# First attention stage: scores in 32-row groups and an order skewed over three sequences; layer weights issued by ScalarE

## What is computed

```
# stage one: one pre-norm attention layer, 16 heads of 8 features, causal
xn = layernorm(x)
q, k, v = xn @ Wq.T, xn @ Wk.T, xn @ Wv.T          # 16 heads x 8
s = q @ k.T / sqrt(8);  s[j > i] = -inf
x = x + (softmax(s) @ v) @ Wo.T
# stage two: six layers on layernorm(x); their result is added back to x
h = layernorm(x)
for l in range(6):
    h = local_attention(shift(h), Wqkv[l], ...) @ Wo[l] + h   # 16 heads x 64, windows of 32
    h = gated_ffn(shift(h), W1[l], b1[l], W2[l], b2[l], ...) + h
x = x + h
```

## Time and profile before

| | |
|---|---|
| median of 3 runs | 4060.95 us |
| profiled execution: its time / its span | 4053.12 / 4051.3 us |
| granted TensorE clock, mean | 0.983 |
| PE busy (share of the span) | 3611.0 us (89%) |
| DVE busy | 3103.8 us (77%) |
| ACT busy | 2876.5 us (71%) |
| POOL busy | 2423.2 us (60%) |
| stage one, until stage two's first PE instruction | 543.15 us |

### The profile page before, as it was taken

One profiled execution on the slowest core, in us unless ns is written; L12 is line 12 of the kernel. 1 busy time (PEld: TensorE's weight loads), 2 busy tenths in 40 slices (PEclk: granted clock), 3 DMA queues, 4 the chain that ended last, 5 costly groups with the idle time before them and its releaser, 6 DMA issues.

```text
span 4051.3 us, 97145 instructions
## 1 busy us (share of the span) xinstructions
PE 3611.0 (89%) x34144; PEld 2541.3 (63%) x34144; DVE 3103.8 (77%) x5305; ACT 2876.5 (71%) x4769; POOL 2423.2 (60%) x1603
## 2 busy tenths in 40 slices
PE   6888869999889999899999899999899998999997
PEld 5666646666566666566666566666666665666665
DVE  4656658888778888778888778888788887888885
ACT  3554447777677777677777677777677776777775
POOL 3222246666666666666666666666566665667663
PEclk9999989999999999999999999999999999999998
DMA  1000001111111111111111111111211111111111
GB/s 56 0 0 0 0 12 34 32 32 34 52 41 31 35 35 35 50 38 35 35 34 36 46 42 35 34 35 35 53 35 35 34 34 44 47 35 35 34 33 48
DMA packets 183169, 136.82 MB, mean 34 GB/s; under 512 B 97612, under 2 KB 135888, under 8 KB 182992
## 3 DMA queue, kind: packets, MB, share of 16 engines
q1 hardware_dynamic: 182992, 134.51, 13.7%
HBM read 19.04 MB, written 2.10 MB: 5 GB/s over the span
## 4 chain that ended last, share of the span: by engine, by line
PE 50%; DVE 14%; ACT 11%; SPq 11%; issue 7%; DMA 5%; POOL 1%; DVEq 0%; ACTq 0%; POOLq 0%
PE ps L1136 9%; PE ps L1177 9%; PE ps L1189 8%; SPq L281 5%; PE ps L1230 5%; PE ps L1215 4%; DMA BD<-area 3%; PE ps L1204 3%; PE ps L1240 3%; SPq L283 3%; DVE area L820 3%; ACT kbd L599 2%; DVE lsum L810 2%; DVE mx L799 2%; DVE area L804 2%
## 5 line engine op out<-in xcount | busy, mean ns | idle before, releaser
L1136 PE MATMUL ps<-Wqkv,xsT 128*128 128x512 f32 x2304 | 1124.0, 611 | 93.1 <-DMA Wqkv<-ffn_Wqkv 44.5
L418 POOL TENSOR_TENSOR area<-area,tab 128x512 f32<-128x512 f32 x384 | 490.1, 1276 | 829.9 <-ACT area L575 829.9
L1136 PEld LDWEIGHTS ps<-Wqkv,xsT 128*128 128x128 f32 x2304 | 406.0, 193 | 432.8 <-issue 337.2
L432 POOL TENSOR_TENSOR area<-area,lsum 128x1024 f32<-128x1024 f32 x192 | 365.3, 1903 | 336.1 <-DVE lsum L813 336.1
L568 ACT ACTIVATE area<-ps 128x1024 f32<-128x1024 f32 x384 | 393.6, 1025 | 202.6 <-PE ps L1136 200.4
L419 POOL TENSOR_TENSOR area<-area,tab 128x512 f32<-128x512 f32 x384 | 490.0, 1276 | 0.0
L426 POOL TENSOR_TENSOR AQb<-AQb,area 128x1024 f32<-128x1024 f32 x192 | 449.8, 2365 | 7.5
L426 POOL TENSOR_TENSOR area<-area 128x1024 f32<-128x1024 f32 x192 | 450.5, 2370 | 0.0
L1177 PE MATMUL ps<-BD,area 128*64 128x128 f32 x6144 | 420.3, 279 | 20.8 <-DMA BD<-area 10.1
L1189 PEld LDWEIGHTS ps<-Wo,area 128*128 128x128 f32 x3072 | 375.9, 193 | 94.5 <-issue 93.6
L1177 PEld LDWEIGHTS ps<-BD,area 128*64 128x64 f32 x6144 | 337.3, 138 | 133.3 <-DMA BD<-area 80.1
(11 more groups left out here) (129 smaller groups left out, 7054.9 us busy)
## 6 DMA issues: line engine op xcount, KB each, us to landing
BD<-area SPq DMA_DIRECT2D x1344, 64.0 KB, 2.0
Vx<-area SPq DMA_DIRECT2D x384, 32.0 KB, 1.9
Wqkv<-ffn_Wqkv SPq DMA_DIRECT2D x18, 512.0 KB, 4.5
BB<-area SPq DMA_DIRECT2D x384, 16.0 KB, 1.8
x2s<-x2s SPq DMA_DIRECT2D x96, 56.0 KB, 2.0
Wo<-ffn_Wo SPq DMA_DIRECT2D x6, 512.0 KB, 4.0
W<-ffn_W SPq DMA_DIRECT2D x6, 341.0 KB
x2s<-x2s SPq DMA_DIRECT2D x96, 7.5 KB, 2.0
```

Source lines behind the costliest of these rows:

```text
L418: pool.tensor_tensor(b4[:, :, 0:h], q4[:, :, h:DH], s4[:, :, 0:h], ALU.mult).then_inc((s_bq, s_bk)[j], 1)
L432: pool.tensor_tensor(p3, p3, lsum[:, 1, :].unsqueeze(2).broadcast_to([P, HEADS, 2 * WIN]), ALU.mult).then_inc(s_pn, 1)
L1136: last = mm(PJ[:, b * 512:(b + 1) * 512], xsT[:, par, t * P:(t + 1) * P], Wqkv[:, w0:w0 + 512], start=True, stop=True)
```

## The change

Stage one:

- k is no longer spread over 128 rows for each head. Four heads share the 32 rows of a group, and POOL writes four copies in place of sixteen (`slotmask`), into one of two halves of `KM`; q is kept twice too. A score product takes its operands from 32 rows of both; two heads of different row groups are done together as a pair j, in two neighbouring banks, one for each head. There are eight pairs in place of four groups. The mask is one product of 256 columns for each head of the pair.
- Maxima are taken by pair (256 and 512 elements), exponentials by pair (four instructions).
- The order is skewed further: pairs 0 to 6 of sequence n and two of its transposed blocks are done in step n, pair 7, the other ten blocks and the value sums in step n+1, and turning, dividing, output product and residual in step n+2. ACT copies four blocks out and DVE eight. The output product goes to `TR[1]`, and pairs and value sums use banks 0 to 5. DVE divides only the eight features of each head, not all 32 columns. The loop is unrolled by two.

The start: `ident` is loaded first; PE no longer waits for `Wap` and `rot`; two large memsets of POOL come after its first spread.

The loads of `Wqkv`: ACT issues them, layer 0's before its first step, the others at the last step of a layer: v after `v_evac(n, 1)`, q after `keep_raw(n, 1, 0)`, k after `keep_raw(n, 1, 1)`.

The core of the diff; in the step functions the removed lines are left out.

```diff
-        KM = area3[:, :].rearrange("p (h k) -> p h k", h=HA)
+        KM = area3[:, 0:2048].rearrange("p (b k n) -> p b k n", b=2, k=4)
...
+        AqT = sb("AqT", [P, 2, SEQ])
...
+            a_step(0, 0, True, False, False)
+            a_step(1, 1, True, True, False)
+            with eng.Fori(0, SEQS // 2 - 1) as k:
+                for odd in range(2):
+                    a_step(eng.snap(2 * k + (2 + odd)), odd, True, True, True)
+            a_step(SEQS, 0, False, True, True)
+            a_step(SEQS + 1, 1, False, False, True)
...
+        BY_ACT = ("00", "10", "01", "02")
+        BY_DVE = ("11", "12", "20", "30", "31", "32", "21", "22")
+
+        SCORE_BANK = {j: 2 * s for j, s in ((7, 0), (0, 1), (1, 2), (2, 0), (3, 1), (4, 2), (5, 1), (6, 2))}
+        VALUE_BANK = 0
...
+        def pair_heads(j):
+            return [(2 * (j % 2) + b, j // 2) for b in range(2)]
...
+            sp.dma_start(ident[:, :], c_ident).then_inc(d_c, 16)
             sp.dma_start(xres[:, 0:early, :], x_rows[:, 0:early, :]).then_inc(d_x, 16)
...
+            for src, dst in ((c_causal, causal_f[:, :]), (c_winmask, wmask_f[:, :, :]), (c_headmask, headmask[:, :])):
...
+                sp.dma_start(Wap[32 * g:32 * g + DA, :, :], wo_rows[g]).then_inc(d_wap, 16)
+            sp.dma_start(xres[:, early:, :], x_rows[:, early:, :]).then_inc(d_x2, 16)
+            sp.dma_start(rot[:, :, :, :], c_rot).then_inc(d_rot, 16)
...
-                if at == SEQS - 1:
-                    need_apart(sp, i_sp, s_pv, (layer + 1) * SEQS * TILES)
-                    load_qkv(layer + 1, 2, d_wv)
-                    need_apart(sp, i_sp, s_pq, (layer + 1) * SEQS * TILES)
-                    load_qkv(layer + 1, 0, d_wq)
-                    need_apart(sp, i_sp, s_pk, (layer + 1) * SEQS * TILES)
-                    load_qkv(layer + 1, 1, d_wk)
...
+            def spread_k(n, par):
                 need(pool, a_ke, n + 1)
...
+                need(pool, a_s, NPAIR * (n - 1))
+                pool.tensor_tensor(KM[:, par, :, :], AkT[:, :].unsqueeze(1).broadcast_to([P, 4, SEQ]),
+                                   slotmask[:, :].unsqueeze(2).broadcast_to([P, 4, SEQ]), ALU.mult).then_inc(a_km, 1)
+
+            def a_step(n, par, head, mid, tail):
+                if head:
+                    spread_k(n, par)
+                    if isinstance(n, int) and n == 0:
+                        pool.memset(kbd[:, :, :, :], 0.0).then_inc(i_zero, 1)
+                        pool.memset(BD[:, :, :, :], 0.0).then_inc(i_zero, 1)
...
+            def load_qkv(l, part, done):
+                col = slice(part * INNER, (part + 1) * INNER)
+                act.dma_start(Wqkv[:, col], wqkv[l][:, col]).then_inc(done, 16)
...
+            def a_exp(n, j):
+
+                need(act, a_mx, NPAIR * n + j + 1)
+                for b, (g, k) in enumerate(pair_heads(j)):
+                    h, bank = 4 * g + k, SCORE_BANK[j] + b
+                    act.activation(E0[:, h, :], ps[:, bank, 0:P], ACT.Exp, bias=nmx[:, 0, h:h + 1])
+                    last = act.activation(E1[:, h, :], ps[:, bank, P:P + SEQ], ACT.Exp, bias=nmx[:, 1, h:h + 1])
                 last.then_inc(a_e, 1)
...
+            def a_step(n, par, head, mid, tail):
+                if mid:
+                    a_values(n - 1)
+                if head:
+                    rsqrt_guess(n, a_lnc, a_lnr, mv, lw)
+                if mid:
+                    a_evac(n - 1, "00")
+                    a_evac(n - 1, "10")
+                if head:
+                    a_x_evac(n)
+                if mid:
+                    a_evac(n - 1, "01")
+                if head:
+                    a_qk_evac(n, par)
+                if mid:
+                    need(act, a_t, NBLK * (n - 1))
+                    a_exp(n - 1, 5)
+                    a_exp(n - 1, 6)
+                    a_exp(n - 1, 7)
+                    a_evac(n - 1, "02")
+                if head:
+                    if mid:
+                        need(act, a_t, turned(n - 1, "02"))
+                    a_exp(n, 0)
+                    a_exp(n, 1)
+                    a_exp(n, 2)
                 if tail:
...
+                    rsqrt_guess(n - 2, b_lnc, b_lnr, mvb, lwb)
+                if head:
+                    a_exp(n, 3)
+                    if mid:
+                        need(act, a_t, turned(n - 1, "22"))
+                    a_exp(n, 4)
 
             act.wait_ge(i_zero, 2)
             act.wait_ge(i_guess, 2)
+            load_qkv(0, 0, d_wq)
+            load_qkv(0, 1, d_wk)
+            load_qkv(0, 2, d_wv)
...
                     v_evac(n, 1, par)
+                    if again:
+                        load_qkv(layer + 1, 2, d_wv)
...
                     keep_raw(n, 1, 0)
+                    if again:
+                        load_qkv(layer + 1, 0, d_wq)
...
                     keep_raw(n, 1, 1)
+                    if again:
+                        load_qkv(layer + 1, 1, d_wk)
...
+            def a_max(n, j):
+
+                bank, (g, k) = SCORE_BANK[j], pair_heads(j)[0]
+                hs = slice(4 * g + k, 4 * g + k + 5, 4)
+                need(dve, a_s, NPAIR * n + j + 1)
+                dve.tensor_reduce(nmx[:, 0, hs], ps[:, bank:bank + 2, 0:P], AX.X, ALU.max, negate=True)
+                dve.tensor_reduce(nmx[:, 1, hs], ps[:, bank:bank + 2, P:P + SEQ], AX.X, ALU.max, negate=True).then_inc(a_mx, 1)
...
+                heads = o3[:, :, 0:DA]
+                dve.tensor_tensor(heads, heads, Arl[:, :].unsqueeze(2).broadcast_to([P, 32, DA]), ALU.mult).then_inc(a_mu, 1)
...
+            def a_step(n, par, head, mid, tail):
+                if head:
+                    moments(n, a_lnc, xres[:, tiles_of(n), :], stats, mv)
+                if tail:
+                    a_gather(n - 2)
+                if head:
+                    a_norm(n)
+                if tail:
+                    a_divide(n - 2)
+                if mid:
+                    a_max(n - 1, 5)
+                    a_evac(n - 1, "11")
+                    a_max(n - 1, 6)
+                    a_evac(n - 1, "12")
+                    a_max(n - 1, 7)
                 if tail:
                     a_residual(n - 2)
+                if mid:
+                    a_evac(n - 1, "20")
+                if head:
+                    a_max(n, 0)
+                    a_max(n, 1)
+                if mid:
+                    a_evac(n - 1, "30")
+                if head:
+                    a_max(n, 2)
+                if mid:
+                    for b in ("31", "32", "21", "22"):
+                        a_evac(n - 1, b)
+                if head:
+                    a_max(n, 3)
+                    a_max(n, 4)
                 if tail:
                     x1_norm(n - 2)
...
+                if isinstance(n, int) and n == 1:
+                    dve.wait_ge(d_x2, 16)
...
+            def a_scores(n, j, par):
+                bank = SCORE_BANK[j]
                 for b in range(2):
...
+                    mm(ps[:, bank + b, 0:3 * P].rearrange("p (a k) -> p a k", a=3)[:, 0:3:2, :], ident_h[:, :],
+                       causal[:, P:2 * P].unsqueeze(1).broadcast_to([P, 2, P]), start=True, stop=False, skip_group_check=True)
+                for b, (g, k) in enumerate(pair_heads(j)):
+                    r = slice(32 * g, 32 * g + 32)
+                    mm(ps[:, bank + b, 0:P], AqT[r, par, 0:P], KM[r, par, k, 0:P], start=False, stop=True, skip_group_check=True)
+                for b, (g, k) in enumerate(pair_heads(j)):
+                    r = slice(32 * g, 32 * g + 32)
+                    last = mm(ps[:, bank + b, P:P + SEQ], AqT[r, par, P:SEQ], KM[r, par, k, :],
                               start=False, stop=True, skip_group_check=True)
...
+            def a_step(n, par, head, mid, tail):
+                old = 1 - par
+                if head:
+                    a_turn(n, mid)
+                if mid:
+                    need(pe, a_te, by_act(n - 1, "10"))
+                    a_turned(n - 1, "01")
+                if head:
+                    a_project(n)
+                if mid:
+                    need(pe, a_te, by_act(n - 1, "01"))
+                    a_turned(n - 1, "11")
+                    need(pe, a_oe, n - 1)
+                    a_scores(n - 1, 7, old)
+                    if head:
+                        need(pe, a_ke, n + 1)
+                    a_turned(n - 1, "12")
                 if tail:
+                    if mid:
+                        need(pe, a_td, by_dve(n - 1, "11"))
                     a_output(n - 2)
                 if mid:
...
+                    need(pe, a_e, NPAIR * n - 2)
+                    need(pe, a_td, by_dve(n - 1, "12"))
+                    a_turned(n - 1, "20")
+                if head:
+                    need(pe, a_km, n + 1)
+                    need(pe, a_qe, n + 1)
+                    a_scores(n, 0, par)
+                if mid:
+                    if tail:
+                        need(pe, a_x1, n - 1)
```

(107 more changed lines are left out.)

234 lines of the change are left out of this document (66 added, 168 removed).

## The result

The changed kernel takes 3852.24 us (median of four runs, 3851.92 to 3856.09), against 4060.78 us before (4055.93 to 4066.61): a ratio of 0.9488, 95% interval 0.9472 to 0.9504, 208 us less. The forecast was 3863 us. In the profiled execution stage one gave back 158 us and stage two 39.

The account below looks back on a forecast made before the run. PE was taken to bound stage one, with waits for Wqkv at stage two's layer ends. 143 us from stage one plus 55 from layer ends, 198, took the 4060.95 us median to 3863; 3835 to 3885 by itself, range to 3928 with rivals.

Parts of the forecast that it names:

- The bound: Stage one: PE bounds it, busy 26.5 us of a 31.5 us sequence, with 5.0 us of waits for copies.
- the slack I gave it: Stage one's new period: PE needs 22.4 us, but 23.0 was taken for a sequence, 0.6 more.
- Scores: Stage one, PE: a pair costs 0.22 masks, 0.75 products, 0.28 mode changes, 1.25 us; eight pairs 10.0 against 13.1.
- my lower bound: Score products of a pair: 0.66 us if the two row groups run side by side.
- The rest of PE: Stage one, PE's transposes, value sums, projections and other work besides scores: 12.4 us a sequence.
- DVE: Stage one: DVE's work rises from 18.8 to 20.5 us a sequence through maxima and copies, less a smaller division.
- The order: Stage one's skewed steps: PE never late by over 0.2 us, margins over DVE 0.2 to 0.5; period 23.0 us.
- the 0.6 us that I added for hand-offs: Stage one's period: allowance for narrow margins between PE at 22.4 and DVE at 20.5 us, giving 23.0.
- Start and end: Stage one: 31 + 24 us beside 15 periods of 23.0; stage two starts at 400 against 543.15, 143 us less.
- Layer ends: Stage two: no PE waits for Wqkv with ACT issuing; 11 us less, five times, 55 us (40 to 60).
- The 0.1 taken off for the four other ends: Layer-end saving: 0.1 us subtracted from each end's 12.1 because the other four waited 0.7 us less on the mean.
- Slow rival: Stage one: the clock falls because 32-row tiles and transposes are lighter work, making the kernel slower; chance 0.04.

Follow-up runs that it names:

- both runs: Changed kernel with layer-end Wqkv loads issued by SP again: 3899.5 us, ratio 0.9616; kernel before with only those loads moved to ScalarE: 4000.32 us, ratio 0.9871.
- the other profiles: Five profiles of the changed kernel or variants of it, with the same start and the same or nearly the same period; stage two begins at 389.0 to 390.1 us.

## Why the prediction was right

- **The bound.** PE bounds stage one: right, and without the slack I gave it.
- **Scores.** A pair was to take 1.25 us and takes 1.17. The bounds were wide, 0.75 for the products looks right to 0.01 (0.22 and 0.11, and 0.43), but that is luck. I thought of loads of 128 columns one behind the other, and the 0.11 is part of the change from whole array to tiles (long products first). The products alone are 0.65, my lower bound, and the change is 0.29 to 0.31 against my 0.28: the error of 0.08 a pair is in the products.
- **The rest of PE**: 21.57 - 8 x 1.17 = 12.2, forecast 12.4.
- **DVE**: 19.5 against 20.5. I had added whole recorded lengths, which overlap from one instruction to the next.
- **The order.** The term that was off is the 0.6 us that I added for hand-offs: no gap is left, and DVE takes 0.8 more without one. With my pair and without the margin the period would have been 22.4; the error of 1.4 us a period is 22 us of stage one.
- **Start and end.** Forecast 55 us beside the 15 periods, measured 385.0 - 15 x 21.57 = 61. I had priced the first step at the high clock. It ran at about half pace until 36.1, 14.6 us after the first masks, where with products over all rows the fast pace came after 3: 7 us. First masks came at 21.5, forecast 20.4: ACT's loads cost 6 us, not 1, and the rest of the start was shorter than I had it. Over the stage the two errors leave 158 us gained against 143; with stage two at 389.0 to 390.1, as in the other profiles, it is 153 to 154.
- **Layer ends.** 52 us by both runs, forecast 55. ACT's issues cost it nothing, forecast 1 us an end; the transfers cost the step before the end some 1 to 2 us, which I had not counted. The 0.1 taken off for the four other ends doesn't follow from their 0.7 us of shorter waits, which is 0.6 on the mean of five; but the traced steps (47.0, 47.0, 47.6, 45.3, 47.3) are on the mean 0.2 shorter than the one I used, so the size held.
- **Slow rival.** It did not come. One row group at a time lost 55 us by a granted clock of 0.50 to 0.52; two side by side ran at 1.00.

Sum: 156 + 52 = 208 against 198. The period alone would have made it 22 us more than forecast; that the sum is off by 10 owes something to the start and the layer ends, which erred the other way.

## What to carry to other kernels

Where an engine bounds a stage and still waits, ask first what its order would give at nearly the same work: here that was three quarters of the gain in the period, and the tiles the smaller part, for here a change into tiles and back costs 0.35 us and pays only where more than that is saved by overlap between two changes. Large transfers that are needed late belong behind the small ones that everything waits for (6 us here), and a load whose issue stands in a long queue of other DMAs belongs on an engine that reaches that point of the program in time (52 us here). Idle products over the whole array, while TensorE has to wait anyway, brought the fast pace here before the row tiles began: the first pair took 1.18 us in place of 2.12.

## What I had not expected of the hardware

- TensorE's granted clock fell to half with PE busy all the time, when score products used one row group of 32 rows at a time (0.50 to 0.52 in the windows from 155 to 172, 329 to 350 and 421 to 438). Two groups side by side kept 1.00 (107.73 to 344.90), but at the start the fast pace came 14 to 23 us after the first masks, where with products over all rows it took 3, and 6 in the kernel before.
- In eleven of the twelve profiles the record of the granted clock reads 1.00 from 3 to 50 us, and in all of them like instructions run at about half their later pace in a part of that time (with the idle products 0.43 us an instruction up to 8.4 us, and 0.22 from 11.5 on).
- Changing between whole array and row tiles costs 0.29 to 0.31 us both ways, with the surplus on the first tile product whatever its length. That products in tiles change the pace of what follows them (transposes 0.49 in place of 0.44) comes on top.
- ScalarE's queue issued `Wqkv`'s loads while an activation ran, the v part 0.15 us into one, so they took nothing from its computing.
